# Interpolated rows: two weighted sets summed by TensorE in the turn, in place of a VectorE addition

## The reference

```python
# layer 0
d  = conv_3x3_stride_2(sx, w_down)          # 256 groups of two channels, 64 x 64 positions
...                                         # clusters, a small mixture: one gate for each image and channel
up = repeat(gate * d + d, 2, axis=1) * w_up
x  = bilinear_up_x2(up) + sx                # rows first, then columns
# layer 1
xP = einsum(x, P)                           # 64 low frequencies of each channel
...                                         # q, k, v products of them, norms over positions
out = WvxP @ (out / lamdv) + out_bias
y   = gamma * out + x
```

## Time and profile before

| | us |
|---|---|
| median of three runs | 3566.51 (3565.6 to 3569.8) |
| the profiled execution | 3571.49 |
| its span | 3569.7 |

### The profile page before, as it was taken

How to read it: one execution, slowest core, us unless ns; L and a number is a source line. 1 busy time by engine, 2 the same in 40 slices (tenths; PEclk the granted TensorE clock), 3 DMA queues, 4 the chain that set the end, 5 groups by cost and what they waited for, 6 DMA issues and landing times. The chain is left out here.

```text
span 3569.7 us, 63832 instructions
## 1 busy us (share of the span) xinstructions
PE 3146.1 (88%) x23398; PEld 2281.7 (64%) x23398; DVE 2855.6 (80%) x3726; ACT 1866.9 (52%) x4385; POOL 1430.4 (40%) x805
## 2 busy tenths in 40 slices
PE   6999999999999969995867989899898988989777
PEld 3555555455554536652446878889787887978777
DVE  4999999899999872203556989888898988889887
ACT  4555555555555534241316656665666656566554
POOL 2676655666666550000002333333333333333333
PEclk9999999999999989596978989999998999999888
DMA  6665665556665634352035989999898999989897
GB/s 256 269 254 228 252 276 231 218 217 240 272 246 229 239 146 174 125 211 66 0 136 200 364 330 361 348 332 360 326 362 331 359 337 347 354 320 360 326 323 286
DMA packets 190891, 946.97 MB, mean 265 GB/s; under 512 B 13505, under 2 KB 13633, under 8 KB 170626
## 3 DMA queue, kind: packets, MB, share of 16 engines
q1 hardware_dynamic: 190594, 943.04, 69.9%
HBM read 638.90 MB, written 301.99 MB: 264 GB/s over the span
## 5 line engine op out<-in xcount | busy, mean ns | idle before, releaser
L1365 PE MATMUL second_o<-second_right,second_left 128*128 128x128 f32 x8192 | 1127.9, 289 | 207.3 <-POOL second_left L1146 126.7
L1146 POOL TENSOR_TENSOR second_left<-second_mid_copy,second_coef_rep 64x1024 f32<-64x1024 f32 x256 | 624.0, 2437 | 1610.9 <-ACT second_mid_copy L1472 1574.6
L1365 PEld LDWEIGHTS second_o<-second_right,second_left 128*128 128x128 f32 x8192 | 1043.5, 203 | 259.5 <-issue 235.8
L217 DVE SCALAR_TENSOR_TENSOR first_partial<-first_x,first_wd,first_partial 128x512 f32<-128x512 f32 (+3 forms) x1200 | 1045.5, 1005 | 0.0
L1607 DVE SCALAR_TENSOR_TENSOR second_x<-second_o,second_shift,second_x 128x512 f32<-128x512 f32 x1024 | 732.9, 739 | 203.5 <-PE second_o L1365 195.7
L290 ACT ACTIVATE first_xT<-first_tp 128x512 f32<-128x512 f32 x1024 | 610.2, 598 | 525.5 <-PE first_tp L317 524.7
L317 PE MATMUL first_tp<-all_const,first_x 128*128 128x128 f32 x4096 | 677.5, 289 | 68.3 <-ACT first_xT L290 36.1
L317 PEld LDWEIGHTS first_tp<-all_const,first_x 128*128 128x128 f32 x4096 | 436.5, 142 | 454.1 <-issue 403.7
L329 PE MATMUL first_freq<-first_xT,first_p 128*64 128x256 f32 x4096 | 668.5, 407 | 9.5
L197 POOL TENSOR_SCALAR first_product<-first_x,first_wd 128x512 f32<-128x512 f32 (+1 forms) x272 | 447.0, 1643 | 494.1 <-ACT first_acc L283 468.8
L1472 ACT ACTIVATE second_mid_copy<-second_mid_t 64x512 f32<-64x512 f32 x256 | 151.7, 593 | 485.0 <-PE second_mid_t L1335 481.6
(11 more groups left out here) (236 smaller groups left out, 2307.8 us busy)
## 6 DMA issues: line engine op xcount, KB each, us to landing
second_x<-in_x SPq DMA_DIRECT2D x256, 1024.0 KB, 11.0
out<-second_x SPq DMA_DIRECT2D x256, 1024.0 KB, 8.6
first_x<-in_x SPq DMA_DIRECT2D x48, 4224.0 KB, 24.6
first_x<-in_x SPq DMA_DIRECT2D x16, 4096.0 KB, 14.5
gather_d<-downsampled SPq DMA_DIRECT2D x24, 2048.0 KB, 12.6
downsampled<-first_acc SPq DMA_DIRECT2D x64, 512.0 KB, 3.5
second_dd<-downsampled SPq DMA_DIRECT2D x64, 512.0 KB, 12.5
first_p<-in_p_cols SPq DMA_DIRECT2D x1, 4096.0 KB
```

What stands on the lines that cost most here:

```text
L217: return nc.vector.scalar_tensor_tensor(out=after[:, rows, left:], in0=tap_window(xt[c], (s, dh, dw), count, row0), scalar=wd[:, t, weight ...
L1146: return eng.tensor_tensor(left[a][rows, odd:HALF:2, :, :].rearrange("p n (t s) g -> p n t s g", t=T), turned[rows, :, :, :].unsqueeze(3). ...
L1365: last = nc.tensor.matmul(ob[n][:, r, :], left[a][:, r, n, :], right[a][:, r, :], start=True, stop=True)
```

## The change

`turn_mid` no longer transposes `mid`. For each output it makes two products with the identity as the moving operand, one with the rows of `mid` and one with the rows of `part` as the stationary operand, into the same place of `mid_t`; the second adds to the first. `interpolate` and its semaphore `interpolated` go, on VectorE, on TensorE and on ScalarE. TensorE waits for `weighted` instead. `part` gets two buffers, like `mid`. `weight` is cut in another way: its argument now picks the row set, not odd or even rows, and the eight activations of `mid` run in the even unit, the eight of `part` in the odd one.

```diff
--- before.py
+++ after.py
@@ -1077,7 +1077,7 @@
         p_sb = sc.sb("p", [P, H, UV])
 
         mid = [sc.sb(f"mid{i}", [P, T, ROWS2, WD]) for i in range(2)]
-        part = sc.sb("part", [P, T, ROWS2, WD])
+        part = [sc.sb(f"part{i}", [P, T, ROWS2, WD]) for i in range(2)]
         zt = [sc.sb(f"zt{i}", [P, ROWS2, UV]) for i in range(2)]
 
         left = [sc.sb(f"left{i}", [P, HALF, TS, P]) for i in range(2)]
@@ -1107,7 +1107,7 @@
         x_in = [[sc.sem(f"x_in{i}_{t}") for t in range(T)] for i in range(XBUF)]
         y_out = [[sc.sem(f"y_out{i}_{t}") for t in range(T)] for i in range(XBUF)]
         dd_in = [sc.sem(f"dd_in{i}") for i in range(DSLOTS)]
-        set_up, weighted, interpolated = (sc.sem(n) for n in ("set_up", "weighted", "interpolated"))
+        set_up, weighted = (sc.sem(n) for n in ("set_up", "weighted"))
         zt_made, multiplied = sc.sem("zt_made"), sc.sem("multiplied")
         mid_turned, zt_turned, mid_copied = sc.sem("mid_turned"), sc.sem("zt_turned"), sc.sem("mid_copied")
         left_made = [sc.sem(f"left_made{i}") for i in range(2)]
@@ -1325,16 +1325,17 @@
 
                     m, a = chunk_of(u), u % 2
                     if a == 0:
-                        pe.wait_ge(interpolated, b * CH2 + m + 1)
+                        pe.wait_ge(weighted, b * CH2 + m + 1 + CHUNK_LEAD)
 
                     pe.wait_ge(left_made[0], b * UNITS + u + FREE)
                     pe.wait_ge(mid_copied, b * UNITS + u + FREE)
                     for n in range(PAIRS):
                         r = a * HALF + 2 * n
                         for t in range(T):
-                            last = nc.tensor.transpose(mid_t[:, n, t, :],
-                                                       mid[m % 2][:, t, r:r + 2, :].rearrange("p h w -> p (h w)"),
-                                                       k("ident"))
+                            for j, rows in enumerate((mid[m % 2], part[m % 2])):
+                                last = nc.tensor.matmul(mid_t[:, n, t, :],
+                                                        rows[:, t, r:r + 2, :].rearrange("p h w -> p (h w)"),
+                                                        k("ident"), start=j == 0, stop=j == 1)
                     last.then_inc(mid_turned, 1)
 
                 def turn_zt(b, u):
@@ -1428,7 +1429,7 @@
                         act.wait_ge(v_made, q + 1)
                         nc.scalar.activation(vt[:, :], st[:, 0:C], ACT.Copy, scale=gam[:, 0:1]).then_inc(vt_made, 1)
 
-                def weight(b, m, e):
+                def weight(b, m, r):
 
 
                     c, n = m % 2, m % CH2
@@ -1436,22 +1437,19 @@
                     def row(i):
                         return min(max(n * DROWS + i, 0), HD - 1) % DRING
 
-                    if e == 0:
+                    if r == 0:
 
                         j = m // CH2 * LOADS + min(n * DROWS + DROWS, HD - 1) // DLOAD
                         if n % 2 == 1 or n == 0:
                             act.wait_ge(dd_in[j % DSLOTS], (b * (LOADS // DSLOTS) + j // DSLOTS + 1) * 16)
 
                         act.wait_ge(mid_turned, (b * CH2 + m) * 2 - 2 + TURN_LEAD)
-                        if m > 0:
-
-                            act.wait_ge(interpolated, b * CH2 + m)
-                    for r in range(2):
+                    for e in range(2):
                         for i in range(DROWS):
                             last = nc.scalar.activation(
-                                (mid[c], part)[r][:, :, 2 * i + 1 - e, :], dd[:, :, row(i + e + r - 1), :],
+                                (mid, part)[r][c][:, :, 2 * i + 1 - e, :], dd[:, :, row(i + e + r - 1), :],
                                 ACT.Copy, scale=row_w[:, 2 * e + r, n * DROWS + i:n * DROWS + i + 1])
-                    if e == 1:
+                    if r == 1:
                         last.then_inc(weighted, 1)
 
                 def place_vt(b, u):
@@ -1482,8 +1480,8 @@
                     for u in range(UNITS):
                         stage(0, u, True)
                     for m in range(2):
-                        for e in range(2):
-                            weight(0, m, e)
+                        for r in range(2):
+                            weight(0, m, r)
                     copy(0, 0)
 
                 def step(b, u, more):
@@ -1492,9 +1490,8 @@
                         stage(b + 1, u)
                     if more or u < UNITS - 1:
                         copy(b, u + 1)
-                    if u % 2 == 1 and (more or m + 2 < CH2):
-                        weight(b, m + 2, 0)
-                        weight(b, m + 2, 1)
+                    if more or m + 2 < CH2:
+                        weight(b, m + 2, u % 2)
 
                 batches(act, step, prologue)
 
@@ -1581,13 +1578,6 @@
                         ch.link(nc.vector.reciprocal(rr[:, :], den))
                         dve.sem_inc(factors_made, 1)
 
-                def interpolate(b, m):
-
-                    c = m % 2
-                    dve.wait_ge(weighted, b * CH2 + m + 1 + CHUNK_LEAD)
-                    nc.vector.tensor_tensor(mid[c][:, :, :, :], mid[c][:, :, :, :], part[:, :, :, :], ALU.add
-                                            ).then_inc(interpolated, 1)
-
                 def frequencies(b, m):
 
                     c, n = m % 2, m % CH2
@@ -1639,7 +1629,6 @@
                             dve.wait_ge(p_in, 16)
                         stage(0, 0, u, ch)
                     take_coef(None, 0)
-                    interpolate(0, 0)
                     assert ch.n == links
                     frequencies(0, 0)
                     scale_odd(0, 0)
@@ -1658,8 +1647,6 @@
                             if u == UNITS - 1:
                                 take_coef(b, 1)
                             scale_odd(b, u + 1)
-                        if n == 2 and u % 2 == 0 and (more or m + 1 < CH2):
-                            interpolate(b, m + 1)
                         if n == 3 and u % 2 == 0 and (more or m + 1 < CH2):
                             frequencies(b, m + 1)
                     if more:
```

## The result

The changed kernel takes 3672.18 us (median of four runs, 3668.53 to 3675.63), the kernel before 3568.16 beside it (3565.6 to 3573.38). The ratio is 1.029, with an interval from 1.027 to 1.030. The profiled execution of after took 3673.16 us, 3671.4 of it span; before had 3569.7.

What follows compares the result with a forecast made beforehand. TensorE bounds units 16 to 23, elsewhere mostly a TensorE-ScalarE-GpSimd loop; 12 added passes (1.34 us) a unit lie on the path: 1781 against 1660 us, +121, start -1.4, so +120 on 3566.5 gives 3687 us, range 3630 to 3750.

Steps and rivals of the forecast that it cites:

- Units with sums: Units 16 to 23 of the first seven batches, TensorE also summing over positions: 7.77 us, TensorE full.
- units without side work: Units with no side work of TensorE: the loop through ScalarE and GpSimd comes last, 4.86 + 1.34 = 6.20 us.
- The plain product costs two passes, not four: Against a rival for the turn: a plain product costs four transposes, giving 4143 us; chance 1%.
- not less than 0.108 us each: Against a rival for the turn: extra passes are cheap, ScalarE's late copy was the true cost, 3488 us; chance 3%.
- VectorE was not late: Against a rival for the last pass: VectorE in order becomes late, units take 0.3 more, 3764 us; chance 8%.
- The 206 us without work: Last pass, 1667 - 1461 us without TensorE work: less than the 344 us of added passes, which would not fit.
- Rival 2: Last pass: the waits swallow the passes and the clock stays up, +50 to +90 us, 3617 to 3657; chance 9%.
- the base of the short unit: Unit without side work before the change: first product to GpSimd's scaling end plus 0.10 us restart, 4.86 us.
- near last only in units 7 to 14: VectorE's addition, 128 of 1.83 us: VectorE is near last only there, with TensorE right behind.
- The one direct term: Start of the last pass: ScalarE no longer waits behind the first addition before the second chunk's weighting, -1.4 us.
- The placements of values: Two at a batch's start on ScalarE, 2.12 us each: TensorE goes on at 7.1 against 6.2, 1.8 us a batch.
- the loads and stores are asked for less: Transfers in the last pass: shortest chunks take 11.6 us now, new ones 12.4 or more, so demand falls.

Runs made afterwards that it cites:

- e11: The changed kernel with only the product of `part` in transpose mode, 12 passes a unit; 3561.18 us, ratio 0.997 to the kernel before.
- e1_split: The changed kernel with transposes and VectorE's addition back, keeping the split weighting and second `part` buffer; 3388.99 us, ratio 0.949 to the kernel before.
- e10: The changed kernel with VectorE's addition kept beside the 16 passes, lower neighbour counted twice; 3693.43 us, ratio 1.035 to the kernel before.
- e5: e1_split without the addition, transposing `mid` alone, so the lower neighbours' share is missing; 3355.78 us, ratio 0.939 to the kernel before.
- e6: The kernel before with two `part` buffers and without ScalarE's wait for the addition; 3571.23 us, ratio 1.000.
- e8_gpsimd_sum: e1_split with the addition moved to GpSimd, half a chunk in each unit behind its scaling; 3380.06 us, ratio 0.946 to the kernel before.

## Why the prediction was right, and where its terms were off

The mechanism was the forecast one in its main points. The turn has 4096 records (2048 for each row set), 0.111 us apart. Units with sums take 7.78 us (7.77 forecast), with TensorE full; units without side work take 6.08 (6.20), ended by GpSimd; the last batch got 21 us shorter (18), with its clock at 1.00; ScalarE's copies come right behind the turns, GpSimd's scalings take 2.36 again, and VectorE's waits for TensorE grew. The plain product costs two passes, not four, as e11's 2040 records against 1020 show, and not less than 0.108 us each. VectorE was not late. The 206 us without work shrank to 58, but the path grew nonetheless, since in the loop the idle comes behind the turn.

**Rival 2 was partly right.** Its two terms, idle time that takes up passes and a clock that stays up, are large: of 344 us of passes 148 went into idle time and 96 are missing from TensorE's busy time (+248), 75 of which e1_split shows with the passes unchanged. That leaves 100, the growth of the pass (1767 for 1667 us). The median, +104, lies 14 us above the rival's range of +50 to +90 and 16 under the forecast, so the time alone would hardly tell them apart; the lengths of the units do.

**What was off: 18 us, nearly all in one term.** Predicted from first product to last unit 1781 us, measured 1762.6. Seven batches gave 1572.9 for 1588, the last 189.7 for 193. The step that failed is the base of the short unit, 4.86 us: I read the loop in unit 3 of batch 4 and took all of it as ScalarE's and GpSimd's. These two rows of the kernel before, from between those of the earlier trace rows, I had passed over:

```profile
2747.08 1.36 DVE L1588 TENSOR_TENSOR second_mid<-second_mid,second_part 128x1024 f32<-128x1024 f32 x1
...
2748.49 0.66 PE L1335 MATMUL second_mid_t<-all_const,second_mid 128*128 128x128 f32 x4
```

VectorE's addition ends at 2748.44, and TensorE's turn starts 0.05 behind it, 1.03 us into the unit. It was an odd unit, whose turn waits for the addition that the change removes. An even one, in e1_split, has its turn at 0.97, a turn of 0.60 and not 0.66 us, and lasts 4.74; 4.74 + 1.34 = 6.08, the unit of after. That is 0.12 us too much for each of 15 units in seven batches and 31 in the last: 136 x 0.12 = 16 us of the 18.

**VectorE's addition was last more often than the prediction said.** It has it "near last only in units 7 to 14, and there TensorE comes right behind". Its mean busy share and its 195.7 us of waiting say nothing of the instant at which the turn waits for it, in most odd units, nor of unit 15, where VectorE is full and the addition costs 1.1 us beside 16 passes and 1.5 beside 4. Measured alone, the addition is worth some 20 us beside 16 passes (e10 against after) and 33 beside 4 (e5 against e1). The one direct term that I took for it, the start, held: from ScalarE's first weighting to the first product the pass takes 13.24 us (1884.53 to 1897.77) where it took 14.80 (1883.93 to 1898.73). The first product comes only 0.96 us earlier, as the stages ahead took 0.6 us longer in that run.

**The two halves cancel.** The sum built after's units from undisturbed ones. Taken apart, it holds 255 turns x 1.34 = 342 us of passes, and so, unsaid, a gain of 222 us from the rest of the change. Measured: -218 us for the rest (e5 against the kernel before beside it: the split 184, the addition the remainder), and +316 for the passes (e5 to after), good to about 5 us. The passes cost 26 us less than 342, 20 of them in the first four, which fell partly beside loads and VectorE's work that came last anyway. So each half is right to within a tenth, and the sum, a difference of the two, is off by 16 of 120.

**Small terms.** The placements of values take a unit to 7.24 us, 7.1 forecast. The buffer, which the prediction gave no term, has none: e6. The DMA engines' share fell from 0.92 to 0.88, and 319 GB/s over the pass for 337 bear out that the loads and stores are asked for less. Two readings of the trace of before do not hold, and nothing in the sum hangs on them. The shortest chunks do not take 11.6 us but 9.6 (units 28 and 29). And TensorE did not come back at half clock at 3398.31: the eight passes there take 1.45 us where 1.13 is the rule, and only the turn behind them is near twice its 0.60 us (1.06, from 3399.56). The granted clock was 1.00 while TensorE stood idle (3395 to 3398), 0.74 from 3398 to 3400 and 0.60 from 3400 to 3403.

What stays open is a part of e8_gpsimd_sum: ahead of the last its batches take 3 us more each than those of e5_no_sum. In batch 4 1.6 us of them lie in units 15 and 16, and no run separates what delays those.

## What to carry to other kernels

A change that bundles a costly move (two row sets through TensorE as plain products) with a good one (splitting a long block of ScalarE's queue) should be taken apart before it is judged: the split alone is worth 5.1%, the whole bundle loses 2.9%. If TensorE is asked to add while it transposes float32 data, use transposes that accumulate: half the passes of a product with the identity. And whether an engine comes last is read at the instant of the wait, instruction by instruction and in each kind of unit, never from its mean busy share; before an instruction is moved earlier, look at what runs on the other engine at that time and at what stands behind it in its own queue.

## What the runs showed of the hardware

- Two float32 transposes into the same place of PSUM, the second not starting anew, add up like products, at one pass each (8 passes a unit, 0.11 us apart: 3448 us). The Trainium skill (Perfetto Trace Analysis, section Transposes) says to take the transpose operation for a logical transpose; the runs agree, with 3448 against 3672 us, and show that it holds even where a sum is wanted.
- One core was served 414 to 417 GB/s of loads and stores together over 144 us (e1_split, e5_no_sum), and 387 over the whole pass of e5_no_sum, where before drew 337 on average over the pass. I had counted on 370.
- An addition of VectorE with two operands in SBUF took 1.35, 1.86 or 2.92 us by where it stood against GpSimd's scaling; nothing else about it was changed. VectorE's frequency rows, 0.68 us elsewhere, took 2.40 us beside a scaling.
